# A decoder layer on one core: the biases of the cross keys and values added by VectorE instead of TensorE and ScalarE, with a new order of work and new PSUM banks

## What is computed

```python
x = x + self_attention(layernorm(x))          # 16 heads of 8, rotary positions, causal softmax
x = x + cross_attention(layernorm(x), ctx)    # no softmax: ((Q K^T) / dk) V, then W_o, residual, layernorm
x = x + moe_ffn(layernorm(x))                 # top 1 of 8 experts, 128 -> 512 -> 128, relu, sigmoid gate

# in the cross attention, the part that is changed
K = ctx @ wk_w.T + wk_b
V = ctx @ wv_w.T + wv_b
```

## Time and profile before

| | |
|---|---|
| median of 3 runs | 698.96 us |
| the profiled execution | 700.01 us |
| its span | 698.1 us |
| TensorE matmul busy | 595.6 us (85%) |
| VectorE busy | 511.2 us (73%) |
| GpSimd busy | 485.7 us (70%) |
| ScalarE busy | 424.5 us (61%) |
| DMA | 35.61 MB, mean 51 GB/s |

### The profile page before, as it was taken

The page is one execution under the profiler, slowest core; times in us unless marked ns, Lnnn a source line. Parts: engine busy times, 40 slices in busy tenths (PEclk is TensorE's granted clock), DMA queues, the critical chain, the costliest instruction groups (busy, mean ns, idle before and its releaser), DMA issues.

```text
span 698.1 us, 27653 instructions
## 1 busy us (share of the span) xinstructions
PE 595.6 (85%) x9104; PEld 453.4 (65%) x9136; DVE 511.2 (73%) x1813; ACT 424.5 (61%) x1154; POOL 485.7 (70%) x899
## 2 busy tenths in 40 slices
PE   3579888988888888888899888987858999999993
PEld 2246656666666566665666666655758989888893
DVE  5766887888788887888788887865455666666662
ACT  1347766767577666767677676764206666666661
POOL 2214676777767776777767776666644898898985
PEclk9999999999999999999999999999558999999997
DMA  4942111111111111111111111100022222222210
GB/s 125 168 137 85 49 38 37 34 40 49 42 33 40 49 33 41 34 40 49 37 37 41 42 40 34 33 23 18 9 61 53 60 61 62 61 64 56 65 51 5
DMA packets 53786, 35.61 MB, mean 51 GB/s; under 512 B 14464, under 2 KB 50049, under 8 KB 53648
## 3 DMA queue, kind: packets, MB, share of 16 engines
q1 hardware_dynamic: 47136, 23.29, 12.9%
q0 software_dynamic: 4352, 8.66, 3.7%
q10 hardware_dynamic: 2160, 1.87, 0.9%
HBM read 24.53 MB, written 9.80 MB: 49 GB/s over the span
## 4 chain that ended last, share of the span: by engine, by line
POOL 31%; DVE 22%; issue 21%; PE 18%; another core or an unknown queue 4%; POOLq 1%; DMA 1%; ACT 1%; DVEq 0%; SPq 0%; ACTq 0%
POOL bs L1612 8%; POOL qk L1480 5%; POOL pay L1542 4%; POOL rs_T L1507 3%; POOL out L1621 3%; DVE t__1 L1104 2%; PE side L659 2%; PE quad L622 2%; DVE shift L1131 2%; PE side L560 2%; DVE stat_T L1082 2%; POOL x L1516 2%; PE quad L614 2%; DVE x L1164 2%
## 5 line engine op out<-in xcount | busy, mean ns | idle before, releaser
L917 ACT ACTIVATE prob<-quad 128x1024 f32<-128x1024 f32 x64 | 65.8, 1032 | 85.9 <-remote 71.8
L1122 DVE TENSOR_REDUCE mx<-quad 128x16 f32<-128x1024 f32 x64 | 77.9, 1220 | 23.4 <-PE quad L588 23.4
L1621 POOL DMA_INDIRECT out<-yo,idi x72 | 77.9, 1081 | 21.1 <-issue 11.7
L901 ACT ACTIVATE ex<-qk,cf 128x512 f32<-128x512 f32 x128 | 81.8, 713 | 7.6 <-POOL qk L1480 7.6
L1570 POOL DMA_INDIRECT expert_rows<-pay,sli x64 | 67.4, 1053 | 21.3 <-issue 15.4
L840 PE MATMUL quad<-w,hT 128*128 x576 | 77.3, 277 | 1.0 <-DVE yb L1424 1.0
L840 PEld LDWEIGHTS quad<-w,hT 128*128 128x128 f32 x576 | 70.6, 193 | 1.8 <-issue 1.8
L1406 DVE TENSOR_SCALAR xh<-rb 128x128 f32<-128x128 f32 x72 | 47.6, 660 | 31.4 <-issue 26.5
L1612 POOL TENSOR_SCALAR bs<-rb 128x128 f32<-128x128 f32 x72 | 57.7, 802 | 10.7 <-DMA rb<-expert_rows 6.7
L1480 POOL TENSOR_TENSOR qk<-t__0 128x512 f32<-128x512 f32 x16 | 20.3, 1268 | 53.6 <-DVE t__0 L1114 48.3
L717 PE MATMUL side<-q,mt 32*32 32x64 f32 x1024 | 37.7, 225 | 19.3 <-issue 18.2
(11 more groups left out here) (195 smaller groups left out, 1708.6 us busy)
## 6 DMA issues: line engine op xcount, KB each, us to landing
rb<-expert_rows SPq DMA_DIRECT2D x72, 68.0 KB
xin<-in_x SPq DMA_DIRECT2D x32, 128.0 KB, 2.1
cin<-in_ctx SPq DMA_DIRECT2D x32, 128.0 KB, 2.2
xr<-in_x SPq DMA_DIRECT2D x32, 128.0 KB, 2.4
w<-in_w1t SPq DMA_DIRECT2D x4, 512.0 KB, 4.5
w<-in_w2t SPq DMA_DIRECT2D x4, 512.0 KB, 5.3
out<-yo,idi POOLq DMA_INDIRECT x72
expert_rows<-pay,sli POOLq DMA_INDIRECT x64
```

What stands on the lines that cost most here:

```text
L901: act(ex[g.par][:, i, :, :].rearrange("p a t -> p (a t)"), qk[g.par][:, :, :].rearrange("p a t -> p (a t)"), ACT.Copy, scale=own4[:, i:i + ...
L917: act(prob[g.par][:, 2 * h_:2 * h_ + 2, :], quad[:, 2 * h_:2 * h_ + 2, :], ACT.Exp).then_inc(*ac_a.done(f"e{h_}"))
L1122: v.tensor_reduce(mx[g.par][:, 2 * h_:2 * h_ + 2, :], quad[:, 2 * h_:2 * h_ + 2, :].rearrange("p r (h k) -> p r h k", k=SQ), AX.X, ALU.max ...
L1621: v.indirect_dma_start(out=o_rows, out_offset=bass.IndirectOffsetOnAxis(ap=idi[b.c % 4][:, 0:1], axis=0), in_=yo[b.c % 4][:, :], in_offset ...
```

## The change

The product of ones with the bias parts (L677) goes, and the products of the context start the accumulation themselves. ScalarE's copy (L929) goes. In its place VectorE adds the bias rows as it takes the bank out, 128x512 floats in one instruction, with the bias read from SBUF and repeated for the two tiles. `values_keys` on TensorE now waits for VectorE's step instead of ScalarE's. The preparation of the bias parts at the start stays as it was. All of the orders (`one(g)` of each engine, SyncE's too), the round in which each step is done for a group, the banks and the table `BEFORE` are replaced. `QUIET` goes from 5 to 4, by which four pieces of preparation for the expert part start one round earlier.

```diff
-        QUIET = 5
+        QUIET = 4
...
-            "cross_keys_values": bank[7],
+            "cross_keys_values": bank[4],
...
-                "affinities": [(ac_r, "xT", 0), (ac_t, "cT", 3), (ac_f, "xT", 5), (dv_r, "i1", -1)],
+                "affinities": [(ac_t, "A", 1), (ac_t, "Q2", 1), (dv_t, "mt", 1), (dv_r, "tot", -1),
+                    (ac_t, "cT", 4), (dv_r, "i1", -1)],
...
                 free(g, "cross_keys_values")
-                mm(BANK["cross_keys_values"], ones_b[:, :], bkv[:, :].unsqueeze(1).broadcast_to((P, J, 2 * D)),
-                   start=True, stop=False)
                 wait(pe, ac_t, g.n, "cT")
                 for j in range(J):
                     last = mm(BANK["cross_keys_values"][:, j * 256:(j + 1) * 256],
-                              cxT[g.par][:, j * P:(j + 1) * P], wc[:, 1:3, :], start=False, stop=j == J - 1)
+                              cxT[g.par][:, j * P:(j + 1) * P], wc[:, 1:3, :], start=True, stop=True)
...
-                wait(pe, ac_t, g.n, "kv")
+                wait(pe, dv_t, g.n, "kv")
...
-            def cross_keys_values(g):
-
-                wait(ac, pe_t, g.n - 2, "gram")
-                wait(ac, pe_t, g.n, "KV")
-                cp(kv2[g.par][:, :, :, :].rearrange("p j a d -> p (j a d)"), BANK["cross_keys_values"][:, :]
-                   ).then_inc(*ac_t.done("kv"))
...
+            def cross_keys_values(g):
+
+                wait(dv, pe_t, g.n - 2, "gram")
+                wait(dv, pe_t, g.n, "KV")
+                v.tensor_tensor(kv2[g.par][:, :, :, :], BANK["cross_keys_values"].rearrange("p (j a d) -> p j a d", j=J, a=2),
+                                br[:, 4:6, :].unsqueeze(1).broadcast_to((P, J, 2, D)), ALU.add
+                                ).then_inc(*dv_t.done("kv"))
...
-                stage(g, 3, scores)
+                stage(g, 2, scores)
...
-                stage(g, 8, alpha)
+                stage(g, 8, alpha)
+                stage(g, 0, stats_x)
...
```

More of the change, by code:

```diff
@@ L392, in decoder_kernel @@
         BANK = {
-            "max_rows": bank[5],
-            "queries_keys": bank[7],
+            "affinities": bank[6],
+            "max_scores0": bank[0],
+            "max_scores1": bank[1],
+            "max_scores2": bank[2],
+            "max_scores3": bank[3],
+            "cross_output": bank[4],
+            "ctx_turned": bank[6],
+            "weighted": bank[7],
+            "x_turned": bank[5],
+            "ranks": bank[6],
+            "x1_turned": bank[4],
+            "values_keys0": bank[5],
+            "values_keys1": bank[6],
+            "max_rows": bank[7],
+            "queries_keys": bank[4],
             "cross_queries": bank[6],
@@ L399, in decoder_kernel @@
             "scores3": bank[3],
-            "projected": bank[5],
+            "projected": bank[7],
             "attended": bank[6],
-            "x2_turned": bank[4],
-            "cross_keys_values": bank[7],
-            "cross_output": bank[5],
-            "values": bank[6],
-            "affinities": bank[4],
-            "max_scores0": bank[0],
-            "max_scores1": bank[1],
-            "max_scores2": bank[2],
-            "max_scores3": bank[3],
-            "values_keys0": bank[6],
-            "values_keys1": bank[7],
-            "weighted": bank[5],
-            "x_turned": bank[4],
-            "x1_turned": bank[7],
-            "ranks": bank[6],
-            "ctx_turned": bank[4],
+            "x2_turned": bank[5],
+            "cross_keys_values": bank[4],
+            "values": bank[5],
         }
@@ L983, in one @@
             def one(g):
-                stage(g, 7, token_ids)
+                stage(g, 7, cross_queries)
+                stage(g, 5, exp, 0)
+                stage(g, 5, exp, 1)
+                stage(g, 8, x2_turned)
+                stage(g, 8, token_ids)
+                stage(g, 7, attended)
+                stage(g, 6, norm_x1)
+                stage(g, 4, values)
+                stage(g, 1, norm_x)
+                stage(g, 3, ctx_turned)
+                stage(g, 7, squares)
+                stage(g, 2, x_turned)
                 stage(g, 4, max_high)
```

139 lines of the change are left out of this document (64 added, 75 removed).

## The result

The changed kernel takes **710.02 us** (median of 4 runs, 709.34 to 712.06), the kernel before, run beside it, 698.56 us (4 runs, 697.45 to 699.39). The ratio is 1.017, 95% interval 1.0144 to 1.0196. The prediction was 687 us, with a range of 664 to 700. The profiled execution took 709.98 us, its span is 708.2, 10.1 more than before. The medians further down take in three executions at a lower granted clock (two of before_again, 798.80 and 897.03 us, and one of the kernel before in the fourth set, 710.32), which the ratios leave out.

The account below looks back on a forecast made before the run. It took a loop through the scatter and its hold as the bound: 5.92 + 2.91 + 2.65 + 2.39 = 13.87 us against 14.28, 27 rounds saving 11 us, plus perhaps 1 us elsewhere: 687 us, range 664 to 700.

Parts of the forecast that it names:

- The hold: In the rounds, the scatter keeps TensorE's signals back until about 2.9 us after its start, costing 1.3 to 1.4 us each.
- The product of ones, ScalarE's copy, the addition: Removing L677 gives up to 0.38 us, L929 alone nothing; VectorE's 0.69 us addition is free while rounds exceed 12.94 us.
- Step 1: From VectorE's first maximum to GpSimd's scatter: 5.92 us against 6.38 before, including 0.18 for GpSimd's start after the reciprocal.
- Step 2: From scatter to first `exp` on ScalarE: 2.91 us, the hold lasting although the scores start about 0.7 us behind the scatter.
- the first rival: The hold goes: `exp` starts 1.98 us behind the scatter, round 12.94 to 13.1 us, 663 to 667 us; chance 0.22.
- Step 3: From `exp` to TensorE's `affinities`, over ScalarE's exponentials, `xpT`, `pay` and `av`: 2.65 us.
- Step 4: From `affinities` to the next first maximum: 2.34 us plus 0.05 for the signal, 2.39 us.
- TensorE's stall: In the small products L717: the stall shrinks from 1.30 us to 0.2 us a round.
- `x1_sum` "isn't held": On VectorE, `x1_sum` comes about 3.8 us behind the scatter, too late for its 1.52 us wait.
- the third rival: VectorE becomes the bound, `x1_sum` still held 1.52 us: 14.46 us a round, 704 us; chance 0.15.
- Ramp and drain: Before and after the full rounds: SyncE's order, `QUIET` and earlier weight loads together change 0, within 2 us.
- "The four pieces fill idle TensorE time": In the drain, the four pieces moved by `QUIET` take only idle TensorE time, within the 0 put for ramp and drain.

Follow-up runs that it names:

- before_again: The kernel before, unchanged, run again on a chip without the hold: 658.16 us, ratio 1.0002.
- after_stash_2: The changed kernel with rows stored plainly by SyncE in the rounds and scattered only after the last round: 829.86 us (other work), 13.02 us a round.
- before_kv: The kernel before with the bias addition on VectorE and nothing else of the change, without the hold: 656.65 us, ratio 0.9983.
- before_kv_2: The same kernel as before_kv, run again on a chip with the hold: 695.52 us, ratio 0.9983 to the kernel before.
- after_kvpe: The changed kernel's orders and banks, but the bias again as product of ones on TensorE and the copy on ScalarE, with the hold: 710.88 us, 1.0225.
- after_off_alpha: after_off with VectorE's reciprocal of the affinity moved up directly behind `slots`, with the hold: 692.73 us, ratio 0.996 to the kernel before.
- off_alpha_2: The same kernel as after_off_alpha, run again in another set with the hold: 693.97 us, ratio 0.9965 to the kernel before.
- after_off: The changed kernel with TensorE's pieces of the experts' offsets moved back behind `ranks`, with the hold: 705.39 us, ratio 1.0147 to the kernel before.
- after: The changed kernel itself, with the whole change, on a chip with the hold: 710.02 us, ratio 1.017 to the kernel before.
- after_again: The changed kernel, unchanged, run again on a chip without the hold: 671.45 us, ratio 1.021 to the kernel before.
- off_alpha_s3: after_off_alpha with GpSimd waiting for the second scores' signal, and `std_x` put ahead of the scatter, with the hold: 735.26 us, ratio 1.0566.

## Why the prediction was wrong, step by step

- **What bounds the kernel.** Right. The hold is worth 14.28 against 12.89 us a round in the kernel before, 1.39; the prediction said 1.3 to 1.4. It comes from the scatter (after_stash_2).
- **The product of ones, ScalarE's copy, the addition.** Right. The addition takes 0.67 to 0.68 us (0.69 estimated). before_kv, before_kv_2 and after_kvpe show that it costs nothing. The Trainium skill's advice to offload from a saturated VectorE (page "Perfetto Trace Analysis", section "Optimizing Scalar/DVE Operations") would have it the other way. In before_kv VectorE is 95% busy in the rounds and nothing is lost, since the work goes to the place where it had idle time.
- **Step 1, first maximum to scatter: 5.92 predicted, 6.46 measured.** This is the step that failed. The instructions took a little less than summed: the reciprocal starts 5.41 us behind the maximum (5.58 in the working). The mistake is the last term, "GpSimd's start after it 0.18". In the earlier trace rows the signals had come in time, and 0.18 is the distance from the engine's own last instruction. The row to read was the one in the earlier trace rows: the scatter idle 1.03 us behind the reciprocal. Behind a signal that comes last it starts 0.88 us late. That one term was 0.70 us too small, and it took away the whole gain that the step was to bring (6.38 to 5.92). after_off_alpha takes the late signal away, and the step is 5.9.
- **Step 2, scatter to `exp`: 2.91 predicted, 2.95 measured.** Right. The scores started 0.07 us behind the scatter, not 0.7, because the scatter was late; off_alpha_2, where they start 0.55 behind, shows that the hold lasts there too (2.90), so the first rival had nothing for it.
- **Step 3, `exp` to `affinities`: 2.65 predicted, 2.87 measured.** Too short by 0.22, and the path was another. The walk had `affinities` wait for ScalarE's copy `av`. TensorE's `values` (L570) waits for `xpT`, 0.75 us, and `affinities` follows it by 0.52; `av`, which ends at 254.69, is there in time.
- **Step 4: 2.39 predicted, 2.30 measured.** Right within 0.1; the 0.05 "for the signal" in it has no row, and none shows it.
- **TensorE's stall and `x1_sum`.** The stall in L717 is 0.43 us (0.2 predicted, 1.30 before). `x1_sum` "isn't held" was wrong: it starts 3.14 us behind the scatter and not 3.8, just when TensorE's signals come. VectorE gets to it late, so 0.26 us of waiting are left (6.1 us between 110 and 400 us, where the kernel before has 30.5), and the third rival, which needed all of it, did not come. Both gains bought nothing in the round.
- **Ramp and drain, 0 within 2 us.** At the edge with the hold (0.4 + 1.6 us), and wrong without it (0.8 + 7.1). "The four pieces fill idle TensorE time" was the fault: in the new order they stand ahead of `affinities` (after_off, with the hold).

The sum: steps 1, 2 and 3 were 0.80 us too short and step 4 was 0.09 too long. The round was predicted at 13.87 and is 14.59, 0.72 more: 27 x 0.72 = 19.4 us. With 2.0 for ramp and drain, and the 1 us that the product of ones was to give there, the 688 us predicted for the profiled execution become 710.4; it took 709.98. The result left the range at the top because no rival held a longer loop over the scatter: the only slower one needed the whole wait at `x1_sum` to stay.

## What to carry to other kernels

Take the delay of an instruction from a row in which the same thing releases it: the scatter's is 0.88 us behind VectorE's signal and 0.17 behind GpSimd's own last instruction. A step for whose result another engine waits should stand as early as its inputs allow; one small instruction, moved up past three steps on VectorE, turned 1.5% slower (after_off) into 0.4% faster (after_off_alpha). When an order is searched, look at what was tucked in beside it (here the pieces in the drain), as it can move from a free place onto the chain.

## What the runs showed of the hardware that was not expected

- An indirect DMA on GpSimd starts 0.88 us behind the end of VectorE's instruction that releases it, with the hold (after) and without (after_again), but 0.16 to 0.18 behind GpSimd's previous instruction where the signals are there. Behind TensorE's scores it was 0.97 (off_alpha_s3).
- Where there is a hold, TensorE's signals don't arrive until 2.8 to 3.1 us behind the start of a scatter: ScalarE's `exp`, or `xpT`, or VectorE's `x1_sum` waits, whichever falls there. The signals of ScalarE and VectorE in the same stretch are on time. The scatter's two DMAs are issued over 2.35 us. The Trainium skill (page "SBUF — State Buffer", section "SBUF: two separate sides") states that PE and ACT wait on no other engine's port; what is waited for here is a signal, and no run shows what keeps it.
- The same program shows this on some chips and not on others, 695 to 699 us against 657, with TensorE's clock at 1.00 in the rounds of both. Each chip was used in one set alone, so it could be the moment as well as the chip. What differs wasn't found.
